# Expert weights of a token tower: eight sets kept on chip and read through registers, in place of a load for each tile

## The reference

```python
    def _L0_ffn_ref(x, W1, b1, W2, b2, Wg, bg):
        B, N, D, E = (8, 2048, 128, 8)
        H = 2 * D
        xf = x.reshape(Bs * Ns, Ds)
        logits = xf @ Wg + bg
        idx = jnp.argmax(logits, axis=-1)
        for e in range(num_experts):
            h = jax.nn.relu(xf @ W1[e] + b1[e])
            y = h @ W2[e] + b2[e]
            out = jnp.where((idx == e)[:, None], y, out)
...
    h = h + _L0_ffn_ref(_layernorm(h, axis=-1), L0_ffn_W1, L0_ffn_b1, L0_ffn_W2, L0_ffn_b2, L0_ffn_Wg, L0_ffn_bg)
```

## Time and profile before

| | us |
|---|---|
| time, median of 3 runs | 2424.78 (2424.73 to 2429.41) |
| profiled execution, first to last instruction (span) | 2515.0 |
| PE busy in it | 2268.3 |
| DVE busy | 1891.7 |
| POOL busy | 1780.9 |
| ACT busy | 1555.5 |

### The profile page before, as it was taken

The page is one execution under the profiler, slowest core; times in us unless marked ns, Lnnn a source line. Parts: engine busy times, 40 slices in busy tenths (PEclk is TensorE's granted clock), DMA queues, the critical chain, the costliest instruction groups (busy, mean ns, idle before and its releaser), DMA issues.

```text
span 2515.0 us, 52301 instructions
## 1 busy us (share of the span) xinstructions
PE 2268.3 (90%) x18308; PEld 1964.4 (78%) x18308; DVE 1891.7 (75%) x5668; ACT 1555.5 (62%) x4990; POOL 1780.9 (71%) x1762
## 2 busy tenths in 40 slices
PE   1579999999999999999999999999999999986775
PEld 0468888888878888888888888888888888776664
DVE  5757778888887878788888888878787888764343
ACT  0246666766767676767677676776777677652322
POOL 5686777778777777777777777787877754344655
PEclk9899999999999999999999999999999999988887
DMA  3011011111110101111111111111111100025665
GB/s 120 26 45 31 24 39 28 41 27 39 29 39 27 41 27 36 31 36 31 36 32 35 34 34 36 29 37 28 40 27 41 27 18 6 6 85 163 185 172 151
DMA packets 73888, 121.75 MB, mean 48 GB/s; under 512 B 20260, under 2 KB 42278, under 8 KB 73520
## 3 DMA queue, kind: packets, MB, share of 16 engines
q0 software_dynamic: 33216, 67.44, 9.8%
q1 hardware_dynamic: 30064, 27.53, 3.8%
q10 hardware_dynamic: 10368, 23.67, 3.3%
HBM read 100.30 MB, written 19.17 MB: 48 GB/s over the span
## 4 chain that ended last, share of the span: by engine, by line
PE 72%; DVE 8%; ACT 6%; POOL 5%; issue 4%; another core or an unknown queue 2%; ACTq 1%; DMA 1%; SPq 0%; DVEq 0%; POOLq 0%
PE psum L1428 63%; PE psum L1449 6%; PE psum L1502 3%; POOL grams L735 2%; POOL gr L770 2%; DVE hid L1222 1%; ACT qm L860 1%; DVE side_n L1173 1%; ACT qkT L858 1%; ACT hid L890 1%; ACT hid L912 1%; ACTq L924 1%; DVE qk L1201 1%; ACTq L922 1%
## 5 line engine op out<-in xcount | busy, mean ns | idle before, releaser
L735 POOL DMA_INDIRECT grams<-gram_table,idx_all x768 | 791.1, 1030 | 187.4 <-issue 182.8
L1428 PE MATMUL psum<-xT,lw 128*128 128x256 f32 x1920 | 483.3, 386 | 0.2 <-ACT xT L846 0.2
L770 POOL TENSOR_TENSOR gr<-ms,con 128x8 f32<-128x8 f32 x192 | 323.9, 1687 | 143.9 <-DVE ms L1227 138.7
L1428 PE MATMUL psum<-lw,hid 128*128 128x129 f32 x3072 | 390.3, 276 | 2.2 <-ACT hid L890 2.1
L746 POOL TENSOR_TENSOR rstd<-ss,con 128x2 f32<-128x2 f32 x320 | 237.9, 746 | 208.3 <-ACT squares L834 201.8
L1428 PEld LDWEIGHTS psum<-lw,hid 128*128 128x128 f32 x3072 | 370.3, 192 | 11.5 <-issue 5.6
L1428 PEld LDWEIGHTS psum<-xT,lw 128*128 128x128 f32 x1920 | 341.9, 193 | 32.9 <-ACT xT L846 0.3
L890 ACT ACTIVATE hid<-psum,par 128x256 f32<-128x256 f32 x768 | 307.6, 486 | 44.9 <-PE psum L1428 41.1
L1428 PE MATMUL psum<-lw,xT 128*128 128x256 f32 (+1 forms) x1536 | 289.3, 331 | 2.9 <-ACT xT L846 2.9
L846 ACT ACTIVATE xT<-psum,par 128x256 f32<-128x256 f32 x384 | 214.1, 562 | 122.8 <-PE psum L1449 114.7
L1449 PE MATMUL psum<-con,xn 128*128 128x128 f32 x1152 | 239.6, 290 | 39.6 <-DVE xn L1134 15.4
(11 more groups left out here) (240 smaller groups left out, 4761.0 us busy)
## 6 DMA issues: line engine op xcount, KB each, us to landing
grams<-expert_w ACTq DMA_DIRECT2D x45, 321.0 KB
grams<-gram_table,idx_all POOLq DMA_INDIRECT x768
grams<-routed_rows SPq DMA_DIRECT2D x80, 132.0 KB
qm<-expert_w ACTq DMA_DIRECT2D x27, 321.0 KB
xb<-x SPq DMA_DIRECT2D x32, 256.0 KB
lw<-layer_w SPq DMA_DIRECT2D x1, 2503.5 KB, 11.8
routed_rows<-row,slot POOLq DMA_INDIRECT x128
grams<-expert_w SPq DMA_DIRECT2D x5, 321.0 KB
```

The lines of the kernel that those rows point to most:

```text
L735: pool.indirect_dma_start(grams[s][:, g, c, :], None, gram_table, bass.IndirectOffsetOnAxis(ap=idx_all[:, g, at:at + 1], axis=0))\
L770: pool.tensor_tensor(gr[s][:, c], ms[s][:, c], const("half")[:, 0:n], ALU.pow).then_inc(y_r[s], 1)
L1428: return pe.matmul(dst, lhsT, rhs, start=start, stop=stop)
```

## The change

All eight weight sets are loaded once, by SP, as soon as the last gathered rows have been summed, into the memory of both `grams` buffers, side by side (`ew`). The four row buffers (`er`) move to other free memory. Nothing loads weights in the loop any more. The second product on PE and the second bias on DVE take their operand at an address that hangs on the expert's number, which each of these engines reads into a register for each tile (`expert_of`). The first matrix, which PE takes as its stationary operand, is copied with its bias by ACT, two copies of 258 columns a unit, into one of two pairs of buffers in `qm` (`up_weights`); ACT reads the expert's number too. The bias columns move next to the first matrix for that. Waits for the schedule and for the weights' arrival stand once before the loop.

```diff
-EW, _ = columns([("w1", EH), ("w2", EB * H), ("b1", EB), ("b2", H)])
+EW, _ = columns([("w1", EH), ("b1", EB), ("w2", EB * H), ("b2", H)])
+UP_COLS = EH + EB
...
-        er = [lent(grams[0], j * TC * ROW, [TC, ROW]) for j in range(SETS)]
-        ew = [lent(grams[1], j * EXPERT_COLS, [EXPERT_COLS]) for j in range(4)] + \
-             [lent(grams[0], SETS * TC * ROW, [EXPERT_COLS])] + \
-             [lent(qm[0], j * EXPERT_COLS, [EXPERT_COLS]) for j in range(3)]
+        free = both_grams[:, :, :, :, :].rearrange("p s g c n -> p (s g c n)")
+        ew = free[:, 0:E * EXPERT_COLS].rearrange("p (e n) -> p e n", e=E)
+        er = [lent(idx_all, 0, [TC, ROW]),
+              sb("er1", [P, TC, ROW])[:, :, :],
+              free[:, E * EXPERT_COLS:E * EXPERT_COLS + TC * ROW].rearrange("p (a n) -> p a n", a=TC),
+              lent(qm[0], 4 * UP_COLS, [TC, ROW])]
+        up_w = [[lent(qm[0], (2 * j + t) * UP_COLS, [UP_COLS]) for t in range(2)] for j in range(2)]
...
+        def expert_of(eng, it, j, t):
+
+            if isinstance(it, int) and it == 0:
+                tile = first_sched[0:1, 1, 2 * j + t:2 * j + t + 1]
+            else:
+                tile = sched[0:1, 1, bass.ds((it - 1) * 2 * SETS + (2 * j + t), 1)]
+            return eng.value_load(tile, min_val=0, max_val=E - 1)
...
+        def weights(ex, name, first=0, width=None):
+
+            at = EW[name].start + first
+            stop = EW[name].stop if width is None else at + width
+            return ew[:, bass.ds(ex, 1), at:stop]
...
+        def expert_up(ex):
+
+            return ew[:, bass.ds(ex, 1), 0:UP_COLS].rearrange("p a n -> p (a n)")
...
-            def load_weights(ex, j, t):
-                sp.dma_start(ew[2 * j + t], expert_w[ex, :, :].rearrange("a p n -> (a p) n")).then_inc(e_w[j], 16)
...
                     load_rows(bass.ds(off, SUB), j, t)
-                    ex = sp.value_load(first_sched[0:1, 1, 2 * j + t:2 * j + t + 1], min_val=0, max_val=E - 1)
-                    load_weights(bass.ds(ex, 1), j, t)
 
             for h in range(2):
                 for s in range(2):
                     sp.wait_ge(acc_step[s][h], pairs * NG)
+            for e in range(E):
+                sp.dma_start(ew[:, e, :], expert_w[e]).then_inc(e_w, 16)
             sp.wait_ge(s_hash_f, FIRST_TILES)
...
                         last = act.activation(eh[j][:, b, c], bank(j % 2, 1 + b)[:, c], ACT.Relu,
-                                              bias=ew[2 * j + t][:, EW["b1"]][:, b:b + 1])
+                                              bias=up_w[j % 2][t][:, EH + b:EH + b + 1])
                     last.then_inc(e_hs, 1)
 
-            def next_weights(it, j):
-
-                act.wait_ge(e_hb, nth(it, SETS, j))
-                act.wait_ge(e_yp, nth(it, SETS, j))
-                act.wait_ge(s_hash_f, SCHEDULED)
+            def up_weights(it, j):
+
+                if not (isinstance(it, int) and it == 0 and j < 2):
+                    act.wait_ge(e_hs, nth(it, SETS * EB, EB * (j - 2) + EB - 1))
                 for t in range(2):
-                    ex = act.value_load(sched[0:1, 1, bass.ds(it * 2 * SETS + (2 * j + t), 1)],
-                                        min_val=0, max_val=E - 1)
-                    act.dma_start(ew[2 * j + t], expert_w[bass.ds(ex, 1), :, :].rearrange("a p n -> (a p) n"))\
-                       .then_inc(e_w[j], 16)
+                    ex = expert_of(act, it, j, t)
+                    last = act.activation(up_w[j % 2][t], expert_up(ex), ACT.Copy)
+                last.then_inc(e_up, 1)
...
                 copy_T(it, 2)
+                up_weights(it, 2)
                 relu(it, 1)
                 copy_T(it, 3)
-                next_weights(it, 0)
+                up_weights(it, 3)
                 relu(it, 2)
                 copy_T(it + 1, 0)
-                next_weights(it, 1)
+                if first:
+                    act.wait_ge(s_hash_f, SCHEDULED)
+                up_weights(it + 1, 0)
                 relu(it, 3)
                 copy_T(it + 1, 1)
-                next_weights(it, 2)
-                next_weights(it, 3)
+                up_weights(it + 1, 1)
...
             def biased(it, j, first=False):
-                dve.wait_ge(e_w[j], (it + 1) * 32)
-                if not first:
+                ex = [expert_of(dve, it, j, t) for t in range(2)]
+                if first:
+                    dve.wait_ge(e_w, 16 * E)
+                else:
                     dve.wait_ge(e_ys, nth(it - 1, SETS, j + 2))
                 for t in range(2):
                     c = slice(SC * t, SC * (t + 1))
                     dve.tensor_tensor(ehb[j][:, c, :], er[j][:, c, 0:H],
-                                      ew[2 * j + t][:, EW["b2"]].unsqueeze(1).to_broadcast([P, SC, H]), ALU.add)
+                                      weights(ex[t], "b2").to_broadcast([P, SC, H]), ALU.add)
...
             def up(it, j, blocks=range(EB)):
                 pe.wait_ge(e_xT, nth(it, SETS, j))
-                pe.wait_ge(e_w[j], (it + 1) * 32)
+                pe.wait_ge(e_up, nth(it, SETS, j))
                 for b in blocks:
                     for t in range(2):
                         c = slice(SUB * t, SUB * (t + 1))
-                        last = mm(bank(j % 2, 1 + b)[:, c], ew[2 * j + t][:, EW["w1"]][:, chunk(b)], exT[j][:, c])
+                        last = mm(bank(j % 2, 1 + b)[:, c], up_w[j % 2][t][:, chunk(b)], exT[j][:, c])
                     last.then_inc(e_hp, 1)
 
             def down(it, j):
+                ex = [expert_of(pe, it, j, t) for t in range(2)]
                 pe.wait_ge(e_hs, nth(it, SETS * EB, EB * j + EB - 1))
                 pe.wait_ge(e_ys, nth(it, SETS, j))
                 for c in range(TC):
                     for b in range(EB):
                         last = mm(bank(j % 2, 3)[:, chunk(c)], eh[j][:, b, chunk(c)],
-                                  ew[2 * j + c // SC][:, EW["w2"]][:, chunk(b)], b == 0, b == EB - 1)
+                                  flat(weights(ex[c // SC], "w2", b * H, H)), b == 0, b == EB - 1)
                 last.then_inc(e_yp, 1)
```

More of the change, by code:

```diff
@@ L46 @@
 EARLY = ((-28.98, -2.51), (18.9, 32.82))
[L47 removed]
+FIRST_UNIT = {"normed": 38.4, "turn": 37.5, "up_weights": 36, "copy_T": 38, "up0": 44.2, "up1": 45.5, "relu0": 46, "biased": 46.2, "relu1": 53,
               "down": 62.5, "result": 64.5}
@@ L299, in tower_program @@
         idx_all = sb("idx_all", [P, NG, rows], U32)
-        grams = two(sb, "grams", [P, NG, CH, H])
+        both_grams = sb("both_grams", [P, 2, NG, CH, H])
+        grams = [both_grams[:, s] for s in range(2)]
         xb = two(sb, "xb", [P, S], I32)
@@ L357, in lent @@
             v = flat_buf[:, at:at + n]
-            v = v if dt == F32 else v.bitcast(dt)
+            v = v if dt == buf.dtype else v.bitcast(dt)
             return v if len(shape) == 1 else v.rearrange("p (a n) -> p a n", a=shape[0])
@@ L483, in tower_program @@
         e_in = each_set("rows_loaded")
-        e_w = each_set("weights_loaded")
+        e_w = sem("expert_weights_loaded")
+        e_up = sem("up_weights_copied")
         e_xn = sem("tile_normed")
@@ L499, in nth, with flat @@
             return it * per + (k + 1)
+        def expert_of(eng, it, j, t):
[8 more added lines that the diff above has]
+            return ew[:, bass.ds(ex, 1), at:stop]
+        def flat(ap):
+            return ap.rearrange("p a n -> p (a n)")
+        def expert_up(ex):
+            return ew[:, bass.ds(ex, 1), 0:UP_COLS].rearrange("p a n -> p (a n)")
         def wait_apart(eng, signal, value, carrier):
@@ L661, in _ @@
                 sp.wait_ge(e_in[j], (units // SETS + 1) * 32)
-                sp.wait_ge(e_w[j], (units // SETS + 1) * 32)
+            sp.wait_ge(e_w, 16 * E)
         @block.gpsimd
@@ L912, in relu @@
                         last = act.activation(eh[j][:, b, c], bank(j % 2, 1 + b)[:, c], ACT.Relu,
[L913 removed]
+                                              bias=up_w[j % 2][t][:, EH + b:EH + b + 1])
                     last.then_inc(e_hs, 1)
[L916 to L920 removed]
+            def up_weights(it, j):
+                if not (isinstance(it, int) and it == 0 and j < 2):
+                    act.wait_ge(e_hs, nth(it, SETS * EB, EB * (j - 2) + EB - 1))
                 for t in range(2):
[L922 to L925 removed]
+                    ex = expert_of(act, it, j, t)
+                    last = act.activation(up_w[j % 2][t], expert_up(ex), ACT.Copy)
+                last.then_inc(e_up, 1)
             def first_unit():
+                yield FIRST_UNIT["up_weights"]
+                act.wait_ge(s_hash_f, FIRST_TILES)
+                act.wait_ge(e_w, 16 * E)
+                act.wait_ge(y_p[0], nth(pairs * LAYERS - 1, 2, 1))
+                up_weights(0, 0)
                 yield FIRST_UNIT["copy_T"]
@@ L934, in _ @@
             main_program(embed, attend, feed, route, first_unit=first_unit)
+            up_weights(0, 1)
             copy_T(0, 1)
```

(7 more changed lines are left out.)

## The result

The changed kernel takes **2432.36 us** (median of 10 runs, 2430.76 to 2434.27) against 2426.55 us for the kernel before in the same series (10 runs, 2423.61 to 2429.41): the ratio is 1.0026, 95% interval 1.0018 to 1.0034. It is slower by about 6 us; the forecast was 2411, faster. The recorded execution took 2432.41 us, with a span of 2430.6.

The account below looks back on a forecast made before the run. The prediction took the expert loop's round as the bound, with GpSimd's stores as a 20.6 us floor: 23.9 us before, 22.0 after, 15 us saved over eight rounds, 1 lost at the start, 2424.78 - 14 = 2411 us; range 2382 to 2442.

Parts of the forecast that it names:

- The share of the trace's waits in timed runs: Expert loop: half of the recording's 6.6 us a round above GpSimd's floor taken as real, so 23.9 us a round before.
- The caution: Whole trace: the recording spans 2515.0 us against 2424.78 timed; at least 90.2 us is in no timed run, place unknown.
- The main stretch can hold little of it if PE is fed at its own pace.: Main program, 200 to 2050 us: 61 ns an instruction on PE, so little of the 90.2 us surplus sits there.
- Register loads on PE: Loop, each second product: two loads and four steps add 1.5 us a unit, 3.95 to 5.5, so 22.0 us a round.
- The argument that the sequencer paces PE: Loop: 61 ns an instruction means the sequencer, not the array, paces PE, speaking against register loads costing nothing.
- Once, the loads of unit 1 stand ahead of the small operations: DVE, once, ahead of the small operations that set the schedule: up to 1.2 us, taken as +1 us.
- the copies, the waits and the moved loads at the end of the main program: First copies and weight waits on ACT and PE, and the eight sets issued together on SP: cost 0.
- the slower one: Loop: PE's register loads make PE set the round, 22.0 us or up to 25.4; 2430 to 2464 us, chance 0.32.
- the third rival: No change: GpSimd sets the loop's round at 20.6 us in both, loads fit PE's waits; 2420 to 2429.6 us, chance 0.20.
- ACT's copies and DVE's loads in the loop at 0: Loop: ACT's eight copies, 3.4 us a round, and DVE's two loads a unit, 1.2 us, are covered; cost 0.
- DMA share: Sign in the changed kernel's profile: DMA share in the loop near 0.25 to 0.3 instead of 0.62.
- PE's clock from 2300 to 2400 us: Sign in the changed kernel's profile: PE's granted clock at 1.00 in the loop.

## Why the prediction was wrong

- **The share of the trace's waits in timed runs: the step that failed.** I took half of the 6.6 us a round by which the recording exceeded GpSimd's floor, since nothing told me how much was real. The runs showed none: a second recording of the same kernel has a loop at 1.311 us a store, and without the weight traffic the time is the same. Where the sum had a round of 23.9 us before and 22.0 after, the recordings have 21.0 and 20.9 (16 steps of 1.311 and 1.306). The saving of 15 us was 0. The caution itself was right, and it gave the sign away: at 90 us the recording was off by more than the effect in question, and 53 us, the most that the loop could save, was less than the surplus to be explained. The likeliest reading was that the loop held all that it could.
- **"The main stretch can hold little of it if PE is fed at its own pace."** Wrong. 61 ns an instruction was the disturbed pace; the undisturbed one is 1850 / (15449 + 15450), 59.9 ns, 1.9% less, and over the whole main program that is about 40 us (the last product that places tokens starts at 2253.60 there and at 2214.56 in the second recording).
- **Register loads on PE.** The size was near (0.61 predicted, 0.52 measured), the place wrong. A unit does not go from 3.95 to 5.5 us: three of four second products stand behind a first product and hide their loads, one shows 1.1 us, so PE's own round is 17.3 us and not 22.0, under GpSimd's 20.6. The argument that the sequencer paces PE, so that nothing hides, was refuted: three of four second products show no gap. The Trainium skill, page "TensorE: Matmul & The Clock Gate", section on the 16 sub-arrays, which gives TensorE a queue of instructions, had it right for the loop: there the rows agree with it as to the hiding, though they don't show how long the queue is.
- **"Once, the loads of unit 1 stand ahead of the small operations": +1 us.** The mechanism was right and the term mis-sized: 6.2 us in the trace, 6.8 in timed runs. I counted one pair of loads on DVE, at 1 us; three pairs show, 0.9 and 1.2 us on DVE and 1.8 on PE ahead of the first second product. The other 2.3 us, products at the lower clock, the sum did not have, and that they follow from the loads is not shown. I also put the copies, the waits and the moved loads at the end of the main program at 0; none of them stands in the chain of the table above.
- **The rivals.** The time fell into the range of the slower one, 2430 to 2464 (and so into the whole range), but by luck, not by that rival's mechanism, which was a longer round. The round of the third rival was right (GpSimd's in both, and the register loads hidden); it missed the start alone.
- **ACT's copies and DVE's loads in the loop at 0: right.** GpSimd's stores are unbroken. DMA share: 0.39 where I had said 0.25 to 0.3, because the share before was also read from the stretched round. PE's clock from 2300 to 2400 us: 0.95 where I had said 1.00.

## What to carry to other kernels

Before a wait in a trace is turned into a saving, compare the span with the timed runs; if the surplus is larger than the saving, record again, or take as the baseline what the engine with the fixed pace would do alone. Where one engine's queue of equal steps ends last (here 142 stores of 1.3 us), only its first step and its gaps count: read the chain up to that first step. Here a pair of register loads (1.03 us on PE) was free behind 1.89 us of queued products, and on DVE in a wait of 1.04 us; behind 0.60 us of transposes and between small dependent steps it cost about its time. Load early, in a place that waits anyway.

## What the runs showed that I had not expected

- One recording's span was some 90 us above the median of the timed runs, about 40 in the main program and 50 in the loop, with waits of up to 7 us for a releaser that the trace doesn't name; the next recording of the same kernel, with the same instructions and the same traffic, was not (2424.4). What stretched the first stays open. The Trainium skill, page "NOTIFIC — the notification-queue block", section 7.1, says that the block that writes the records holds back what feeds it rather than lose a record inside the block. That would be a possible cause; that a second recording has no stretch shows that recording alone does not bring it about, and no run here shows more.
- 232 GB/s of traffic at 0.80 of the DMA engines, beside GpSimd's stores, hardly touches the pace at which they are issued: 1.311 us each with it, 1.307 in the same kernel without the weight loads. They land later: DVE waits up to 4.6 us for one, against 1.5 in the changed kernel.
- The first register loads of a stretch took up to 0.55 us (DVE, 555 ns) where the median in the loop is 0.30.
